# Graph-convolution gathers: one-hot tiles shared between ScalarE and VectorE, and made there by a two-tensor compare

## What is computed

```python
def gcn_conv(x, edge_index, W, b, num_nodes):
    ...
    dinv = jnp.where(deg > 0, jax.lax.rsqrt(deg), 0.0)
    norm = dinv[src_f] * dinv[dst_f]
    h = x @ W
    msg = h[src_f] * norm[:, None]
    out = jax.ops.segment_sum(msg, dst_f, num_segments=num_nodes)
    return out + b
```

## Time and profile before

| what | us |
|---|---|
| median of 3 runs | 39,790.85 (39,516.95 to 39,814.47) |
| the profiled execution | 39,946.08 |
| its span, first to last instruction | 39,944.3 |
| DVE busy over the span | 16,251.5 (41%) |
| PE busy | 14,169.2 (35%) |
| POOL busy | 21,803.8 (55%) |
| ACT busy | 2,594.5 (6%) |
| c1: first one-hot tile to last chunk | 14,393 to 18,470 |
| c2: the same | 18,850 to 22,817 |

### The profile page before, as it was taken

The page is one execution under the profiler, slowest core; times in us unless marked ns, Lnnn a source line. Parts: engine busy times, 40 slices in busy tenths (PEclk is TensorE's granted clock), DMA queues, the critical chain, the costliest instruction groups (busy, mean ns, idle before and its releaser), DMA issues. The chain is left out here.

```text
span 39944.3 us, 271822 instructions
## 1 busy us (share of the span) xinstructions
PE 14169.2 (35%) x71326; PEld 10724.1 (27%) x71326; DVE 16251.5 (41%) x34865; ACT 2594.5 (6%) x3901; POOL 21803.8 (55%) x20450
## 2 busy tenths in 40 slices
PE   1111100111111036665566533423433343166664
PEld 1000000100000035554455412212222222144443
DVE  2333337222222546665566522323332332344443
ACT  0000000000000000000000000000000000033331
POOL 4655640455455246664676555564455555377773
PEclk5555555555555567776787756656666666577775
DMA  2000013111111211111111110000000000100001
GB/s 43 13 12 11 13 9 123 15 18 18 17 20 18 95 37 29 28 28 20 25 29 29 23 10 9 11 10 8 8 11 9 9 11 8 50 16 14 14 14 47
DMA packets 1088987, 932.94 MB, mean 23 GB/s; under 512 B 580668, under 2 KB 1031892, under 8 KB 1063892
## 3 DMA queue, kind: packets, MB, share of 16 engines
q1 hardware_dynamic: 440100, 695.25, 5.8%
q0 software_dynamic: 646368, 201.76, 5.3%
q10 hardware_dynamic: 1872, 28.29, 0.2%
HBM read 497.08 MB, written 426.83 MB: 23 GB/s over the span
## 5 line engine op out<-in xcount | busy, mean ns | idle before, releaser
L1100 POOL DMA_INDIRECT messages<-se_M,se_rstage x2625 | 2951.3, 1124 | 4001.5 <-DVE se_M L1463 3209.2
L1100 POOL DMA_INDIRECT messages<-pe_M,pe_rstage x2625 | 3129.7, 1192 | 1097.5 <-issue 792.2
L493 POOL DMA_INDIRECT g1g_G<-tab,g1g_stage x3125 | 3130.6, 1002 | 1038.0 <-issue 1021.1
L493 POOL DMA_INDIRECT se_G<-tab,se_stage x3125 | 3016.8, 965 | 1038.9 <-issue 1026.0
L493 POOL DMA_INDIRECT g2g_G<-tab,g2g_stage x3125 | 2953.3, 945 | 1041.0 <-issue 1022.0
L999 DVE SCALAR_TENSOR_TENSOR g2gh_junk<-g2gh_pB,g2gh_src_f,earlier 128x128 f32<-128x128 f32 (+4 forms) x2625 | 1453.8, 614 | 3827.6 <-remote 3062.9
L1408 DVE TENSOR_TENSOR se_V<-se_pTV,s_b 128x160 f32 (+1 forms) x625 | 202.7, 324 | 6708.2 <-remote 3856.6
L493 POOL DMA_INDIRECT c2c_G<-tab16b,c2c_stage x2125 | 2567.2, 1208 | 659.0 <-issue 640.0
L493 POOL DMA_INDIRECT c1c_G<-tab,c1c_stage x2125 | 2549.1, 1200 | 658.9 <-issue 641.5
L1011 PE MATMUL g2gh_pB<-ident_b,src_lo 128*128 128x128 bf16 x2625 | 665.1, 286 | 5191.0 <-issue 3725.7
L711 PE MATMUL g1gh_acc<-g1gh_oh_hi,g1gh_oh_lo 128*128 128x100 bf16 x6250 | 634.1, 284 | 4733.2 <-DVE g1gh_oh_hi L692 2182.6
(11 more groups left out here) (594 smaller groups left out, 34505.6 us busy)
## 6 DMA issues: line engine op xcount, KB each, us to landing
scans<-g1w_W SPq DMA_DIRECT2D x25, 3187.5 KB, 9.9
c1cm_row<-match SPq DMA_DIRECT2D x500, 128.0 KB
c2cm_row<-match SPq DMA_DIRECT2D x500, 128.0 KB
edges<-g2g_G SPq DMA_DIRECT2D x25, 2062.5 KB, 6.4
g2w_G<-edges SPq DMA_DIRECT2D x25, 2062.5 KB, 11.6
scans<-g2w_W SPq DMA_DIRECT2D x25, 2062.5 KB, 7.3
g1g_G<-tab,g1g_stage POOLq DMA_INDIRECT x3125
g2g_G<-tab,g2g_stage POOLq DMA_INDIRECT x3125
```

The lines of the kernel that those rows point to most:

```text
L493: g.indirect_dma_start(out=G[b][:, t, :], out_offset=None, in_=table, in_offset=bass.IndirectOffsetOnAxis(ap=stage[b][:, t:t + 1], axis=0) ...
L1100: g.indirect_dma_start(out=view, in_=M[b][:, DC + t, :], in_offset=None, out_offset=bass.IndirectOffsetOnAxis(ap=stage[b][:, t:t + 1], axis=0)
```

## The change

Of the 13 one-hot tiles of a block, VectorE makes the first MV = 8 and ScalarE the last 5. VectorE's compare no longer takes the node number of the partition as a per-lane scalar, but as a second tensor (the same value read 512 times). ScalarE makes a tile in two steps: Abs of (row minus number), then Relu of (1 minus that), with its own two half-precision buffers `off`. ScalarE's instruction order is written out so that the tiles of block m+1 come ahead of the table copy of side group m. PE waits for both makers before it multiplies.

```diff
+MV = 8
...
             @block.scalar
             def _(a):
-                side.scalar(a)
+                a.wait_ge(match.split, 1)
+                a.sem_inc(match.warmed, 2)
+                side.scalar(a, 0)
+
+                def chunk(i, b, j):
+                    match.warm(a, i, 0)
+                    for m in range(max(NB, side.groups)):
+                        if m + 1 < NB:
+                            match.warm(a, i, m + 1)
+                        if m < side.groups:
+                            side.scalar(a, i * side.groups + (m + 1))
+                over_chunks(a, chunk)
...
-    def scalar(a):
-
-        with a.Fori(0, NCH * groups + 1) as n:
-            a.wait_ge(added, n + 1)
-            a.activation(table[:, :], pT[:, 0:NT], ACT.Copy).then_inc(copied, 1)
+    def scalar(a, n):
+
+        a.wait_ge(added, n + 1)
+        a.activation(table[:, :], pT[:, 0:NT], ACT.Copy).then_inc(copied, 1)
...
+        self.off = [c.sb(f"{name}_off{b}", [P, BE * P], F16) for b in range(2)]
+        self.minus = c.sb(name + "_minus", [P, MJ])
...
+        self.measured, self.warmed = c.sem(name + "_measured"), c.sem(name + "_warmed")
...
+        ch(v.tensor_scalar(self.minus[:, :], self.first[:, :], -1.0, None, ALU.mult))
...
-        for j in range(MJ):
-            v.tensor_scalar(self.hot[m % 2][:, j, :], self.row[:, 0, m * BE * P:(m + 1) * BE * P],
-                            self.first[:, j:j + 1], None, ALU.is_equal).then_inc(self.heated, 1)
+        for j in range(MV):
+            v.tensor_tensor(self.hot[m % 2][:, j, :], self.row[:, 0, m * BE * P:(m + 1) * BE * P],
+                            self.first[:, j:j + 1].to_broadcast([P, BE * P]), ALU.is_equal).then_inc(self.heated, 1)
+
+    def warm(self, a, i, m):
+
+        n = i * NB + m
+        a.wait_ge(self.rows_in[m], i * 32 + 32)
+        a.wait_ge(self.multiplied, n + 1)
+        at = slice(m * BE * P, (m + 1) * BE * P)
+        for t, j in enumerate(range(MV, MJ)):
+            off = self.off[(m * (MJ - MV) + t) % 2]
+            a.wait_ge(self.warmed, n * (MJ - MV) + (j - MV + 1))
+            a.activation(off[:, :], self.row[:, 0, at], ACT.Abs, bias=self.minus[:, j:j + 1]).then_inc(self.measured, 1)
+            a.wait_ge(self.measured, n * (MJ - MV) + (j - MV + 1))
+            a.activation(self.hot[m % 2][:, j, :], off[:, :], ACT.Relu, bias=1.0, scale=-1.0).then_inc(self.warmed, 1)
...
-        pe.wait_ge(self.heated, n * MJ + MJ)
+        pe.wait_ge(self.heated, n * MV + MV)
+        pe.wait_ge(self.warmed, n * (MJ - MV) + (MJ - MV + 2))
```

## The result

The changed kernel takes 42,910 us (42,725 to 43,422) against 39,791 (39,517 to 39,814): ratio 1.079, interval 1.071 to 1.087, 3,119 us more. The forecast was 41,750 with an upper end of 42,700. The profiled execution is the longest of its four (43,421.9), and the ratio leaves it out.

A forecast was written before the change was run, and what follows sets the result against it. DVE's list was taken to pace the blocks, POOL's gathers plus tail the chunk. Chunk 137.2 - 3.1 saved + 67 of PE crawl = 201.1, +42.5 for 46 chunks = +1,955: 41,750 us; range 39,200 to 42,700.

The forecast's parts named there:

- under cover: ACT's five tiles, 7.5 to 8.0 us, lie under a block of about 12 us and cost nothing.
- rival 2: ScalarE switches function tables for Abs and Relu in each block: +4,150 us, 43,900 in all; chance 0.05.
- crawls: PE beside undisturbed gathers in c1 and c2: one instruction per 1.4 us, a block 151 us for 12 of work.
- let through: PE, whatever the stage, gets hardly more than one instruction per gather when POOL's gathers follow each other undisturbed.
- the onset: Start of PE's crawl in a chunk of c1 or c2, put at 40 us behind the first gather.
- a mean cycle of 1.41 to 1.46 us: POOL's gathers beside the changed blocks, against 1.59 before; nearer to the 1.39 at which g1g mostly crawled.
- my 1.8 us per gather: Each POOL gather in the 6.2 us run of two-tensor compares waits for every third compare's end.
- 67: Loss in us per chunk from PE's crawl: 73 us of crawl at 0.92 lost per us.
- 201.1: Forecast chunk in us, 137.2 - 3.1 + 67, against 158.6 before; taken for c1 and c2 alike.
- onset at 11 us ..., 90 us lost: Bad bound, with POOL undisturbed: crawl starts 11 us in, +65.5 us a chunk, 42,800 us in all.
- The threshold: Gather cycle on POOL, some 1.45 us, above which PE was to stay free and the block loop decide.
- rival 1: PE stays free and gathers take 122 us: -9 to -12 us a chunk, 39,310 us in all; chance 0.27.

The follow-up runs named there:

- e4: Changed kernel plus 12 more compares with a number per lane in every block on VectorE, result unread; 42,985 us, ratio 1.082.
- e2: Kernel before with VectorE making all 13 tiles by the two-tensor compare and ScalarE none; 44,304 us, ratio 1.121.
- e6: Changed kernel with a copy of 128 numbers per lane and one wait on POOL between every two gathers; 39,666 us, ratio 0.969.
- e16: Changed kernel, unchanged, run again in a free group; 32,572 us against 32,726 for the kernel before, ratio 0.996.
- e14: Changed kernel with a copy of 8 numbers on POOL behind every second gather, in a crawling group; ratio 0.979.
- e5: Changed kernel with a copy of 8 numbers per lane on POOL between every two gathers, in a crawling group; 39,743 us, ratio 0.969.
- e9: Changed kernel with a copy of 8 numbers on POOL behind every second gather, in a free group; ratio 0.986.
- e11: Kernel before, unchanged, run for its trace in a free group; 32,937 us, ratio 1.000.

## Why the prediction was wrong in size

**What held.** Compares of two tensors start 0.60 us apart (eight in 4.90 us in e4). ACT's five tiles lie under cover, 5 x (0.709 + 0.631) = 6.7 us against the 7.5 to 8.0 expected; rival 2 is out. POOL is freed: 0.958 us for a gather. PE then crawls, with 1.35 us per instruction against the 1.4 taken from the earlier trace rows; the wait is "remote", in front of the product, not at block 9. That PE is "let through" slowly was taken from windows that count records; at two of the waits that I read so (g1g, block 9) PE's records were already complete, and it is the finished work that came late. e2 and e6 show that this is cause and not company. One condition was luck: the prediction rests on a trace of a crawling occasion and says nowhere that there are others, and both kernels were timed on such a one. On a free one the sign is the other (e16).

**The step that failed** is the onset: "the crawl begins about 35 us behind the first gather, 40 if the first chunk ... is left out", together with "a mean cycle of 1.41 to 1.46 us" for the gathers until then. In the chunk shown it begins 13 to 20 us behind the first gather and ends only some 8 us behind the last. Over all chunks of c1 the first 20 gathers of a set are 1.29 us apart, the others 1.25. The two-tensor compares do not hold POOL up to speak of: my 1.8 us per gather beside them was built on two gathers of the earlier trace rows. The last chunk of c1 has no gathers beside it and takes 106 us from first to last product; with the 24 to the next first product a chunk without loss is 130, where I had 134. The chunks in the middle take 229.7: the loss is 99.6 us, not 67. That is 229.7 - 201.1 = 28.6 us more per chunk than forecast in c1, and 224.8 - 201.1 = 23.7 in c2: 23 x 52.3 = 1,203 us, and the forecast was 1,160 short. The bound "onset at 11 us ..., 90 us lost" was near. It gave 42,800, still 110 below the 42,910 measured, and I took the range to 42,700: the range cut off the end that its own bound named.

**The threshold** of 1.45 us (rival 1's condition) does not sort the runs. e4 has a mean cycle of 1.46 us in c1 and e14 of 1.47, but their waits sum to 1,748 and 998 us; the mean is lowered by the crawl itself, since a waiting VectorE disturbs nobody.

**Rival 1** asked for 39,310, 1.2% less. In a free group it is the right mechanism, and 0.4% the one gain measured (e16). Its gain was sized on the 133.6 us of gathers plus 25 of tail; in e16 the blocks and their own tail set the chunk.

**What stays open:** why PE is starved beside gathers on some occasions and not on others with the same program. The gathers' pace (1.25 us) and length (0.94 us) are the same on both. How much pause PE needs, and in which pieces, isn't settled either, nor how far the hold-ups by VectorE share in what e5 and e6 gain.

## What to carry to other kernels

Before making an engine faster, look whether its slowness paces another one: here POOL, freed by cheaper compares, starved PE, and the kernel lost 7.9% with less work on the engine that set its blocks. Where an engine's pace collapses in one stretch of a trace, take the worst stretch as the bound and let the range reach it. If such a coupling is found, pace the culprit itself: one short copy behind every second gather with the changed tiles beat the kernel before in a crawling group by 2.1% and in a free one by 1.4% (e14 0.979, e9 0.986); the copy in all four gather stages gave 0.921 where PE crawled and 1.016 where it did not. And where a long wait is marked "remote", compare the record of the instruction that it asks for with the moment of release, before reading that engine's records as its pace.

## What the hardware showed unexpectedly

- PE can be slowed to one instruction in 1.35 us while POOL issues indirect gathers 1.25 us apart, though its idle time there is "issue", no wait that the profile shows; it is back at nine per us once they end (windows above). Its records can then run up to 87 us ahead of what frees the other engines.
- The same program took 39,764 and 32,937 us in two groups of runs, with gathers equally fast. Between its first trace (39,946 us) and that of e11, 100 us of g2g hold 80 against 320 PE instructions.
- A copy of 8 numbers per lane on POOL lasts 0.2 us. One between every two gathers puts them 1.34 us apart instead of 1.25 where VectorE is silent, and 1.52 on average; with it PE is let through in most chunks (e5).
- A gather that starts beside compares can last through a whole row of them: 8.40 us in the kernel before, whose first two blocks' 26 compares with a number per lane run in one row, and 10.06 in e4, through eight compares of two tensors and the twelve with a number behind them. In e2, which has compares of two tensors only, the longest was 2.58.
